# Softmax denominators of a gated cross-attention layer: three accumulating transfers per query half and one matmul group, in place of four matmul groups

## The reference

```python
# per batch and head, t = 1024 queries, s = 1024 keys
dot = jnp.einsum('bhdt,bhds->bhts', q, k) / math.sqrt(HEAD_DIM)
dot = mask * dot - (1.0 - mask) * NEG
amap = jax.nn.softmax(dot, axis=-1) * mask
out = jnp.einsum('bhts,bhds->bhdt', amap, v)
x = x + jnp.tanh(g_xattn[0]) * out.reshape(b, HEADS * HEAD_DIM, t)
# then: layernorm, rounding to fp8, product with W2, gate, residual
```

## Time and profile before

| | |
|---|---|
| time, median of 3 runs | 2536.92 us (2534.54 to 2538.61) |
| the profiled execution: span from the first to the last instruction | 2538.4 us |
| first stage, before the loop over quads | about 500 us |
| PE busy | 2479.6 us, 98% of the span |
| POOL busy | 1642.1 us, 65% |
| DVE busy | 1986.1 us, 78% |
| ACT busy | 1392.0 us, 55% |
| mean rate of all transfers | 123 GB/s |

### The profile page before, as it was taken

One profiled execution on the slowest core, in us unless ns is written; L12 is line 12 of the kernel. 1 busy time (PEld: TensorE's weight loads), 2 busy tenths in 40 slices (PEclk: granted clock), 3 DMA queues, 4 the chain that ended last, 5 costly groups with the idle time before them and its releaser, 6 DMA issues.

```text
span 2538.4 us, 40565 instructions
## 1 busy us (share of the span) xinstructions
PE 2479.6 (98%) x13177; PEld 1380.4 (54%) x13177; DVE 1986.1 (78%) x3259; ACT 1392.0 (55%) x2606; POOL 1642.1 (65%) x1259
## 2 busy tenths in 40 slices
PE   7999999999999999999999999999999999999997
PEld 5888888874444444444444444444444444444442
DVE  6767667776788888888888888888888888888885
ACT  3333333315666665666666666666665666666664
POOL 2333333426777777777777777777777777777775
PEclk9999999999999999999999999999999999999999
DMA  6766666653444444444444444444444444444411
GB/s 239 256 244 239 237 237 237 215 183 88 94 97 97 100 102 94 96 91 94 91 97 93 91 91 91 91 91 90 99 91 92 95 99 100 97 98 99 101 47 55
DMA packets 241807, 313.48 MB, mean 123 GB/s; under 512 B 75000, under 2 KB 142648, under 8 KB 241624
## 3 DMA queue, kind: packets, MB, share of 16 engines
q1 hardware_dynamic: 230776, 275.56, 43.2%
q10 hardware_dynamic: 10848, 35.66, 3.9%
HBM read 199.83 MB, written 101.38 MB: 119 GB/s over the span
## 4 chain that ended last, share of the span: by engine, by line
PE 88%; DVE 6%; issue 3%; DMA 1%; POOL 1%; ACT 0%; SPq 0%; DVEq 0%; POOLq 0%; ACTq 0%
PE bank L863 20%; PE bank L848 20%; PE bank L893 19%; PE bank L878 17%; PE bank L904 8%; PE bank L941 4%; DVE part_max L1146 3%; PE bank L933 1%; POOL pair_sum L398 1%; DMA q_st<-qx_scr 0%; DVE y L101 0%; DMA w_nat<-in_L_xattn_Wk_dram 0%; DMA v_scr<-stage 0%; DVE isnan L100 0%; DVE x_raw L1046 0%
## 5 line engine op out<-in xcount | busy, mean ns | idle before, releaser
L398 POOL TENSOR_TENSOR pair_sum<-probs 128x512 f32<-128x512 f32 x1020 | 1279.6, 1287 | 430.8 <-ACT probs L715 430.8
L1146 DVE TENSOR_REDUCE part_max<-bank 128x1 f32<-128x512 f32 x2048 | 1283.0, 682 | 346.4 <-PE bank L878 338.1
L715 ACT ACTIVATE probs<-bank 128x512 f32<-128x512 f32 x2048 | 1071.3, 603 | 655.8 <-PE bank L863 647.4
L863 PE MATMUL bank<-q_st,k_st 100*128 100x512 f32 x2048 | 875.4, 429 | 5.2 <-ACT probs L715 5.2
L878 PE MATMUL bank<-k_st,q_st 98*128 98x512 f32 x2048 | 814.0, 397 | 8.7 <-DVE part_max L1146 6.2
L863 PEld LDWEIGHTS bank<-q_st,k_st 100*128 100x128 f32 x2048 | 386.5, 189 | 513.2 <-issue 270.8
L893 PE MATMUL bank<-probs,v_t 128*32 128x512 f32 x4096 | 546.3, 605 | 0.0
L878 PEld LDWEIGHTS bank<-k_st,q_st 98*128 98x128 f32 x2048 | 388.7, 190 | 112.6 <-DVE part_max L1146 8.7
L389 POOL TENSOR_TENSOR stage_lo<-stage,stage_hi 128x512 fp32r<-128x512 f32 x128 | 185.4, 1473 | 139.5 <-ACT stage_hi L661 138.6
L904 PE MATMUL bank<-pair_sum,ones 128*32 128x512 f32 x2040 | 266.4, 594 | 0.0
L661 ACT ACTIVATE stage_hi<-stage 128x512 fp32r<-128x512 f32 x128 | 80.2, 632 | 205.7 <-DVE stage L1010 143.1
(11 more groups left out here) (112 smaller groups left out, 1969.1 us busy)
## 6 DMA issues: line engine op xcount, KB each, us to landing
k_st<-k_scr SPq DMA_DIRECT2D x96, 512.0 KB
q_st<-q_scr SPq DMA_DIRECT2D x192, 256.0 KB
c_raw<-in_ctx_dram ACTq DMA_DIRECT2D x32, 512.0 KB, 7.1
k_scr<-stage_hi SPq DMA_DIRECT2D x64, 256.0 KB, 2.5
k_scr<-stage_lo SPq DMA_DIRECT2D x64, 256.0 KB, 2.8
v_scr<-stage SPq DMA_DIRECT2D x64, 256.0 KB, 2.9
q_scr<-stage_hi SPq DMA_DIRECT2D x64, 256.0 KB, 2.3
q_scr<-stage_lo SPq DMA_DIRECT2D x64, 256.0 KB, 2.5
```

Of the source, the lines that this page charges most:

```text
L398: nc.gpsimd.tensor_tensor(pair_sum[:, r % 2, h], probs[:, a, h], probs[:, a + 1, h], ALU.add).then_inc(pair_done, 1)
L715: nc.scalar.activation(probs[:, c % PR, h, :], s_bank_of(n, k)[:, :], ACT.Exp).then_inc(exp_done, 1)
L863: nc.tensor.matmul(s_bank_of(n, k)[:, :], k_st[p][0:KS, h, j * P:(j + 1) * P], q_st[p][0:KS, th, h, :], start=True, stop=True).then_inc(sc ...
L1146: nc.vector.tensor_reduce(part_max[:, th, sh, at:at + 1], x_bank_of(n, "tile", k)[:, :], AX, ALU.max).then_inc(max_done, 2)
```

## The change

The four pair sums of a half get four buffers: the first goes into one of two `pair_sum` buffers, the other three into `stage`, `stage_hi` and `stage_lo`. After each of these three, POOL issues a transfer of 128 x 2048 floats (1 MB) that adds the buffer to the first one in place (`accum_op=ALU.add`). The second and the third transfer each wait for the one before to have landed. PE then has one group of ones-matmuls a half, on the finished sum: at slot 47 for half 0 and at slot 15 of the next period for half 1. In the last half of the program, two pairs are chained, and the fourth pair is summed by PE from `probs` as before. ACT's copies move from slots 12 and 44 to 16 and 48.

```diff
+            first_sum = [pair_sum[:, 0], pair_sum[:, 1]]
+            next_sum = [stage[:, :, :], stage_hi[:, :, :].bitcast(F32), stage_lo[:, :, :].bitcast(F32)]
...
                     def add_pair(n, r):
-                        a = 2 * r % PR
-                        if counted(SJ * n + r - 1):
-                            pool.wait_ge(den_done, SJ * n + r - 1)
+                        a, g, i = 2 * r % PR, TH * n + r // 4, r % 4
+                        if i == 0:
+                            to = first_sum[g % 2]
+                            if counted(g - 1):
+                                pool.wait_ge(den_done, g - 1)
+                        else:
+                            to = next_sum[i - 1]
+                            if counted(16 * g):
+                                pool.wait_ge(added[i - 1], 16 * g)
                         for h in range(QH):
...
+                    def add_to_first(n, r):
+
+                        g, i = TH * n + r // 4, r % 4
+                        pool.wait_ge(pair_done, QH * (SJ * n + r + 1))
+                        if i > 1:
+                            pool.wait_ge(added[i - 2], 16 * (g + 1))
+                        pool.dma_start(first_sum[g % 2], next_sum[i - 1], accum_op=ALU.add).then_inc(added[i - 1], 16)
...
                                 add_pair(n, r)
+                                if r % 4 > 0:
+                                    add_to_first(n, r)
...
-                    def denominators(m, r):
-                        th, i = r // 4, r % 4
-                        if i == 0:
-                            if counted(2 * m + th):
-                                pe.wait_ge(den_copied, 2 * m + th)
-                        pe.wait_ge(pair_done, QH * SJ * m + QH * (r + 1))
+                    def denominators(m, th):
+                        g = TH * m + th
+                        if counted(g):
+                            pe.wait_ge(den_copied, g)
+                        part = 2 if (m, th) == (LAST, TH - 1) else 3
+                        pe.wait_ge(added[part - 1], 16 * (g + 1))
...
+                        if k == 47 and real(n):
+                            denominators(n, 0)
+                        if k == 15 and ordinary(n - 1):
+                            denominators(n - 1, 1)
```

More of the change, by code:

```diff
@@ L187, in flamingo_gated_layer @@
         pair_done = sem("pair_done")
+        added = [sem(f"added{i}") for i in range(3)]
         pv_done = sem("pv_done")
@@ L390, in batch, with wait_stage_free @@
                                                     ALU.subtract).then_inc(qk_lo, 1)
+                    def wait_stage_free():
+                        for i in range(STG):
+                            pool.wait_ge(v_stored[i], 16 * B * (GV // STG))
+                            pool.wait_ge(qk_stored[i], 32 * B * (2 * GK // STG))
                     def add_pair(n, r):
-                        a = 2 * r % PR
-                        if counted(SJ * n + r - 1):
-                            pool.wait_ge(den_done, SJ * n + r - 1)
+                        a, g, i = 2 * r % PR, TH * n + r // 4, r % 4
[7 more added lines that the diff above has]
+                                pool.wait_ge(added[i - 1], 16 * g)
                         for h in range(QH):
                             pool.wait_ge(exp_done, NSLOT * n + 2 * QH * r + QH + h + 1)
-                            nc.gpsimd.tensor_tensor(pair_sum[:, r % 2, h], probs[:, a, h], probs[:, a + 1, h],
+                            nc.gpsimd.tensor_tensor(to[:, h], probs[:, a, h], probs[:, a + 1, h],
                                                     ALU.add).then_inc(pair_done, 1)
+                    def add_to_first(n, r):
[4 more added lines that the diff above has]
+                        pool.dma_start(first_sum[g % 2], next_sum[i - 1], accum_op=ALU.add).then_inc(added[i - 1], 16)
                     def weigh(m):
@@ L723, in copy_den @@
                     def copy_den(m, th):
[L724 removed]
+                        act.wait_ge(den_done, TH * m + th + 1)
                         if counted(16 * (2 * m + th)):
@@ L763, in period @@
                                 copy_o(n - 1, 1)
-                            if k == 12 and ordinary(n - 1):
+                            if k == 16 and ordinary(n - 1):
                                 copy_den(n - 1, 1)
@@ L769, in period @@
                                 copy_o(n, 0)
-                            if k == 44 and real(n):
+                            if k == 48 and real(n):
                                 copy_den(n, 0)
@@ L895, in times_v @@
                         last.then_inc(pv_done, 1)
-                    def denominators(m, r):
-                        th, i = r // 4, r % 4
-                        if i == 0:
-                            if counted(2 * m + th):
-                                pe.wait_ge(den_copied, 2 * m + th)
-                        pe.wait_ge(pair_done, QH * SJ * m + QH * (r + 1))
+                    def denominators(m, th):
[4 more added lines that the diff above has]
+                        pe.wait_ge(added[part - 1], 16 * (g + 1))
                         for h in range(QH):
-                            last = nc.tensor.matmul(d_bank[D * h:D * (h + 1), :], ones[:, :], pair_sum[:, r % 2, h, :],
-                                                    start=(i == 0), stop=(i == 3))
+                            last = nc.tensor.matmul(d_bank[D * h:D * (h + 1), :], ones[:, :], first_sum[g % 2][:, h, :],
+                                                    start=True, stop=(part == 3))
                         last.then_inc(den_done, 1)
```

17 lines of the change are left out of this document (7 added, 10 removed).

## The result

| | before | after |
|---|---|---|
| time, median | 2535.97 us (2534.54 to 2538.61) | 3258.68 us (3251.39 to 3265.27) |
| profiled span | 2538.4 us | 3257.4 us |
| mean granted TensorE clock | 0.994 | 0.869 |

The ratio is 1.2843, with a 95% interval of 1.2818 to 1.2868. The kernel became slower, as forecast, but by 723 us and not by the 242 us that the sum gave (2778 us).

What follows compares the result with a forecast made beforehand. PE was taken to bound the kernel before, POOL after: 61.4 + 7 = 68.4 us a quad against 60.9, 233 us over 31 quads; 2538.4 + 233 + 8.5 - 1.5 = 2778 us. Own range 2600 to 3150, 8 in 10: 2440 to 3400.

Steps and rivals of the forecast that it cites:

- POOL's loop: POOL's work and landing waits over a quad: 61.4 us, with 7 for shared DMA engines 68.4, against 60.9 before.
- D: POOL's time to issue one transfer: taken as 1.0 us, bounds 0.4 and 1.3.
- L: Time from the start of a transfer's issue until POOL or PE can go on: taken as 8.5 us.
- The burst: k and q loads at slot 0 saturate the DMA engines for 18.5 us, delaying new transfers: 7 us a quad.
- this second wait is covered: PE's wait for k and q at slot 19 hides behind its wait of about 10 us at slot 15.
- Rival 2: Quick transfers, but k and q late at slot 19: PE waits 2 to 4 us a quad; 2450 to 2510 us; chance 0.13.
- while POOL is the bound: POOL sets the quad's time, so half of the slow-clock cost after PE's waits is covered.
- 4L + 27.4: Time of a quad in us when POOL is late, before sharing with the loads: 61.4 at a landing of 8.5.
- the 65 to 72 forecast: Sign of being right: the distance between two bursts of loads, in us.
- the gain of 164 us: 191 groups of ones-matmuls removed from PE at 0.86 us each, all on the path: a quad would take 55.7 us.
- the clock: PE's granted clock may drop to 0.50 after long waits: a few us more, not in the sum.

Runs made afterwards that it cites:

- e_copy: The changed kernel with plain copies of the same size in place of the adding transfers, same waits: 2931.77 us, ratio 1.1557.
- e_free: The changed kernel with its 1 MB adding transfers going into each pair's own buffer, none waited for within the half: 3243.78 us, ratio 1.2777.
- b_free: The kernel before, all groups kept, plus 192 adding transfers of 1 MB of unused buffers, none waited for within a half: 3197.83 us, ratio 1.2598.
- e_none_dve: The changed kernel without its transfers and with DVE's extra normalization steps cut to 64 elements: 2412.23 us, ratio 0.9509.
- e_small: The changed kernel with all transfers and waits, but each transfer moving 64 KB in place of 1 MB: 2579.43 us, ratio 1.016.
- e_none: The changed kernel without its transfers, PE's one group a half summing the first pair alone: 2486.73 us, ratio 0.9795.
- g_free_nb_s: The changed kernel with transfers not waited for within a half, k and q loads cut, DVE's subtraction at slot 19: 2687.31 us, ratio 1.0587.
- f_nb_s_e: The changed kernel with k and q loads cut, DVE's subtraction at slot 19, POOL's two long operations ahead of transfer 3: 2915.29 us, ratio 1.1489.
- e_slot19: The changed kernel with DVE's subtraction moved from slot 11 to slot 19, nothing left out: 3278.09 us, ratio 1.2912.
- f_nb_e: The changed kernel with k and q loads cut and POOL's two long operations ahead of transfer 3, subtraction at slot 11: 3024.18 us, ratio 1.1918.
- b_link: The kernel before, with POOL adding pair 5 into pair 6's place by four additions and one group less a quad, no transfer: 2630.9 us, ratio 1.0364.

## Why the prediction was right in its direction and wrong in its size

**Right: more is paid than gained, and the transfer's own terms.** The direction came out right partly by luck: what sets the time of the changed kernel is the late loads of k and q, and not the length of POOL's loop, from which slower was forecast. D was taken as 1.0 us; POOL's issues take 0.87 us in the median. L was taken as 8.5 us: from the start of the issue to landing it is 6.9 us at the least and 9.8 in the median from 700 to 3100. Counting an addition as twice the bytes was a little high: it takes 1.66 times the engine time of a copy. Of the two rules of the Trainium skill that the prediction weighed, the trace does not bear out the one of "DMA: Bandwidth & Descriptors" for an adding transfer (an estimate of 4.4 us; a plain copy's shortest landing in `e_copy` is 4.4 us). It is near the one of "Collectives: The Full Stack", that the addition halves the rate: 6.9 us at the least, the rule's estimate being 6.8, though the engine time gives 1.66 and not 2.

**Wrong, the step that failed: "The burst".** The prediction put it as a share of the DMA engines on POOL's side, +7 us a quad on POOL's loop, and on the other side had the first part of k and q land 13.9 us after slot 0, "in the changed kernel 0.9 us earlier" needed, and closed with "this second wait is covered". The runs show the reverse. k and q let PE go on 34.7 us after slot 0, and `e_free` and `b_free`, in which nobody waits for a new transfer, take 3243.78 and 3197.83 us. The working left out the engines' own account: three 1 MB additions are issued between 1.7 us before the first load and the start of slot 19 (at 1721.84, 1731.14 and 1742.17), 3 x 5.4 = 16.2 us of all 16 engines. Nearly all other quads show the same three, a few us earlier or later. Two smaller readings in this step were off as well. The issue at 1299.88 of the earlier trace rows, taken as slot 0, is the last of three; the first stands at 1299.01:

```profile
1299.01 1.30 SPq L498 DMA_DIRECT2D k_st<-k_scr  x3
```

And the first part lands later than 13.9 us after it even with no large transfer beside it: in `e_none_dve` at about 16 us in the quads in which PE hardly waits for it, and at up to 17.4 us in the others. It is needed 1315.88 - 1299.01 - 0.9 = 16.0 us after it in the changed kernel, so it had next to no slack, where the prediction had 1.2 us. An estimate from these rows, 16.0 to 17.4 with 16.2 on top, is 32.2 to 33.6 us, close to the 33 to 35 measured; the rest is not settled, and SP's own issues, 3.82 us for the three of k in place of 1.30, are one candidate. Rival 2 had this mechanism, at 2 to 4 us a quad and only under quick transfers; it counted part of one transfer where three came in.

**Wrong: "while POOL is the bound".** POOL's loop of 68.4 us a quad was not the bound: two bursts are 83.8 us apart in the mean, outside the 65 to 72 forecast, while 4L + 27.4 with the measured median L of 9.8 gives 66.6, and POOL stood 19.43 us in the quad shown for exponentials. With the shortest L, 6.9, that sum is 55.0, under PE's 55.7. `e_small` keeps each wait, with shorter landings, and costs 93 us over `e_none`; `g_free_nb_s` against `f_nb_s_e` shows that the waits for landings are worth 228 us when nothing hides them. In the changed kernel they are hidden: `e_free` is only 15 us quicker.

**Wrong: the gain of 164 us, "all of it is on the path".** It was 50 us (`e_none`). A group's distance of 0.86 us was read rightly, but DVE's extra steps stood in the same slots and took its place; with these shortened it is 125 us in all (`e_none_dve`), and the last 39 stay unexplained. This term was off by 114 us, and its error made the forecast too low.

**Not in the sum: the clock.** It was named and left at a few us. `e_none` and the changed kernel have the same matmuls. PE's busy time is 2351.3 and 2591.3 us, its idle time 134.7 and 666.1 us. So of 771 us more, some 225 to 240 are matmuls that take longer, granted 0.50 after waits as in the windows above, and the rest are waits. (The trace of `e_none` lacks the records of 61 matmuls of L962, which leaves PE's busy time there up to some 15 us too short.)

**Not foreseen: DVE held by POOL.** The subtraction of two SBUF operands took 1.25 us and now takes 8.0. The Trainium skill, "SBUF — State Buffer", in its section on who interferes with whom, says that such an instruction contends with a GpSimd one that reads SBUF. The trace agrees: the 8.35 us lie beside a row of eight POOL additions, which POOL, late after its waits, now does one after another. Alone it is not a cost here (`e_slot19`, which takes it away, is 19 us slower than the changed kernel); it is worth 109 us where the loads are gone (`f_nb_e` against `f_nb_s_e`).

The costs do not stand side by side: each is hidden behind another until that one is gone. Taking away the loads gives 213 us, then the subtraction and the order 130, then the waits for landings 228, and what is left to `e_none` is 201. Another order would give other shares: the waits for landings are worth 15 us with the loads there and 228 without them.

**Open.** Why the first part of k and q gets no more of the engines than this is not shown. The packets of the two queues differ in size (q1: 275.56 MB in 230776, 1.2 KB each; q0: 200.29 MB in 27504, 7.3 KB each), which would favour q0 if the engines took turns by packet, but no run changed the packets alone. These are means over the whole program. How the last 201 us split among small transfers, DVE and the rest is open too.

## What to carry to other kernels

Before moving work onto the DMA engines, add up their time in the window before each load that something waits for (here 3 x 5.4 us in front of a load with next to no slack), not over the period, where the share of 0.43 looked free. A saving on the busiest engine is worth only what the second engine's work in the same slots leaves of it. Run the bare traffic beside the old kernel first: here `b_free` alone would have settled the idea.

## What the runs showed of the hardware

- An adding transfer of 1 MB within SBUF, issued by GpSimd, takes 5.4 us of all 16 DMA engines, a copy 3.25; the issue holds POOL 0.87 us, that of a copy 0.57. The shortest landings are 6.9 and 4.4 us.
- Other transfers land later in the changed kernel: `v_t` in 8.7 us in place of 4.1, and `out_dram` (512 KB) in 7.7 in place of 2.6, both against the earlier trace rows.
- One DVE instruction with two SBUF operands waited through a row of POOL additions (8.35 us, ending one microsecond after the eight of them), though POOL's row is made of separate instructions.
- Beside 15 us of POOL additions in a row, two row-maximum steps of DVE on 16 elements a partition took 1.2 us each, in place of 0.17 (`b_link`).
- With waits like the 7.27 and 8.60 us of the quad shown, PE's mean granted clock over the program fell from 0.994 to 0.869.
